# FFN down products on one core: W2's two parts as one 256-column operand, and two sums per row tile on VectorE

## What is computed

```python
logits = xt @ Wr + br
top_p, top_idx = jax.lax.top_k(jax.nn.softmax(logits, axis=-1), 2)
weights = top_p / top_p.sum(axis=-1, keepdims=True)
xn = (xt - mu) * jax.lax.rsqrt(var + LN_EPS)
xe = xn[None, :, :] * ln_g[:, None, :] + ln_b[:, None, :]
h = jax.nn.gelu(jnp.einsum('end,edh->enh', xe, W1) + b1[:, None, :], approximate=False)
y = jnp.einsum('enh,ehd->end', h, W2) + b2[:, None, :]
out = (weights[:, :, None] * sel).sum(axis=1)      # sel: y of the two chosen experts
```

## Time and profile before

| | us |
|---|---|
| median of 3 runs | 1040.82 (1039.2 to 1045.29) |
| the profiled execution | 1043.44 |
| its span | 1041.4 |
| TensorE busy (matmul) | 791.3 |
| VectorE busy | 631.6 |
| ScalarE busy | 583.3 |
| GpSimd busy | 560.8 |

### The profile page before, as it was taken

How to read it: one execution, slowest core, us unless ns; L and a number is a source line. 1 busy time by engine, 2 the same in 40 slices (tenths; PEclk the granted TensorE clock), 3 DMA queues, 4 the chain that set the end, 5 groups by cost and what they waited for, 6 DMA issues and landing times. The chain is left out here.

```text
span 1041.4 us, 25571 instructions
## 1 busy us (share of the span) xinstructions
PE 791.3 (76%) x7318; PEld 665.7 (64%) x7319; DVE 631.6 (61%) x2144; ACT 583.3 (56%) x1167; POOL 560.8 (54%) x581
## 2 busy tenths in 40 slices
PE   0667798687778377629278999999968899899995
PEld 0455688466668266512067877888757788787874
DVE  3555511877450588863257777878745666666663
ACT  1467752788332355231056766777646667676763
POOL 0756600443127788677725555656554555555554
PEclk9999999566579567555579999999998999999998
DMA  9497511566102244715123333333323333434441
GB/s 238 104 271 243 162 53 44 185 179 199 41 14 78 95 126 135 233 46 193 51 79 117 120 103 121 115 116 112 109 66 108 109 112 111 113 109 116 115 116 35
DMA packets 123849, 124.78 MB, mean 120 GB/s; under 512 B 22233, under 2 KB 91120, under 8 KB 123796
## 3 DMA queue, kind: packets, MB, share of 16 engines
q1 hardware_dynamic: 89476, 80.65, 27.3%
q0 software_dynamic: 15296, 34.64, 9.5%
q10 hardware_dynamic: 19024, 8.86, 3.0%
HBM read 77.40 MB, written 49.09 MB: 121 GB/s over the span
## 5 line engine op out<-in xcount | busy, mean ns | idle before, releaser
L1026 DVE TENSOR_TENSOR AB<-AB 128x512 f16<-128x512 f32 x280 | 192.1, 686 | 73.0 <-ACT AB L694 68.7
L528 POOL DMA_INDIRECT row_dram<-B x140 | 143.7, 1027 | 112.6 <-DVE B L1032 77.0
L528 POOL DMA_INDIRECT out<-B x140 | 139.6, 997 | 117.5 <-DVE B L1032 92.1
L691 ACT ACTIVATE AB<-ps 128x512 f16<-128x512 f32 x280 | 168.2, 601 | 41.2 <-PE ps L1208 40.6
L1225 PE MATMUL ps<-PPb,AB 128*128 x1120 | 185.3, 219 | 0.0
L1226 PE MATMUL ps<-PPb,AB 128*128 x1120 | 185.1, 219 | 0.0
L694 ACT ACTIVATE AB<-ps 128x512 f32<-128x512 f32 x280 | 169.2, 604 | 0.0
L1206 PE MATMUL ps<-B,PPb 128*128 128x256 f16 x560 | 154.5, 276 | 0.5 <-issue 0.5
L1207 PE MATMUL ps<-B,PPb 128*128 128x256 f16 x560 | 154.0, 275 | 0.0
L1208 PE MATMUL ps<-B,PPb 128*128 128x256 f16 x560 | 154.0, 275 | 0.0
L1228 PE MATMUL ps<-PPb,AB 128*128 x1120 | 153.9, 219 | 0.0
(11 more groups left out here) (218 smaller groups left out, 1620.9 us busy)
## 6 DMA issues: line engine op xcount, KB each, us to landing
B<-row_dram SPq DMA_DIRECT2D x70, 264.0 KB
B<-row_dram SPq DMA_DIRECT2D x70, 136.0 KB
rows<-in_x SPq DMA_DIRECT2D x32, 256.0 KB, 5.3
rows<-in_L_conv_protein_pair SPq DMA_DIRECT2D x16, 512.0 KB, 4.9
g_dram<-work ACTq DMA_DIRECT2D x32, 256.0 KB, 3.3
work<-g_dram SPq DMA_DIRECT2D x32, 256.0 KB, 2.8
ABT<-in_x SPq DMA_DIRECT2D x32, 256.0 KB, 3.0
ABT<-in_L_conv_protein_pair SPq DMA_DIRECT2D x16, 512.0 KB, 4.8
```

Source lines behind the costliest of these rows:

```text
L528: pool.indirect_dma_start(out_rows if second else row2_dram, bass.IndirectOffsetOnAxis(ap=Rw[:, u, b, at:at + 1].bitcast(u32), axis=0), Rw ...
L691: act.activation(Hp[:, hs, 0, :], ps[HB[hs]][:, :], ACT.Gelu, scale=1.0 / SCALE)
L1026: dve.tensor_tensor(Hp[:, hs, 1, :], Hf[:, q, :], Hp[:, hs, 0, :], ALU.subtract).then_inc(h_parts[q], 1)
```

## The change

The two parts of W2 are laid side by side for every piece k, so that one slice of 256 columns holds high and low. In the down block, for each k and half, the high part of the hidden layer is loaded once and streams all 256 columns into the whole width of 256 of bank 4 + b: the first 128 columns collect high x high, the second 128 high x low. The low part of the hidden layer streams the first 128 columns as before. That is 16 products in place of 24; the b2 products stay, now behind the first product of their bank. The bank then holds two sums. VectorE adds the first to the row in mix, as before, and the second in a new mix_low; y_high orders the two, and y_done is now released by mix_low. The order of VectorE's stages changes: both mix ahead of the second h_low, both mix_low behind it.

```diff
-        W2h = flat[:, 4096:8192].bitcast(f16).rearrange("p (e r k d) -> p e r k d", e=NE, r=2, k=HC)
+        W2h = flat[:, 4096:8192].bitcast(f16).rearrange("p (e k r d) -> p e k r d", e=NE, r=2, k=HC)
...
-        y_psum, y_done = ([sem(f"{name}{b}") for b in range(HALVES)] for name in ("y_psum", "y_done"))
+        y_psum, y_high, y_done = ([sem(f"{name}{b}") for b in range(HALVES)] for name in ("y_psum", "y_high", "y_done"))
...
-                        a = act.activation(W2h[:, e, 0, :, :], W2s[:, e, :, :], ACT.Copy, scale=SCALE)
+                        a = act.activation(W2h[:, e, :, 0, :], W2s[:, e, :, :], ACT.Copy, scale=SCALE)
...
-                i = dve.scalar_tensor_tensor(W2h[:, e, 1, :, :], W2s[:, e, :, :], SCALE, W2h[:, e, 0, :, :], ALU.mult, ALU.subtract)
+                i = dve.scalar_tensor_tensor(W2h[:, e, :, 1, :], W2s[:, e, :, :], SCALE, W2h[:, e, :, 0, :], ALU.mult, ALU.subtract)
...
                 dve.scalar_tensor_tensor(Rw[:, u, b, 0:D], ps[4 + b][:, 0:D], Rw[:, u, b, w:w + 1], Rw[:, u, b, 0:D],
+                                         ALU.mult, ALU.add).then_inc(y_high[b], 1)
+
+            def mix_low(n, u, second, b):
+
+                dve.wait_ge(y_high[b], n + 1)
+                w = WHI if second else WLO
+                dve.scalar_tensor_tensor(Rw[:, u, b, 0:D], ps[4 + b][:, D:2 * D], Rw[:, u, b, w:w + 1], Rw[:, u, b, 0:D],
                                          ALU.mult, ALU.add).then_inc(y_done[b], 1)
...
-                            (2, lambda n, u, second: h_low(n, u, 1)), (3, lambda n, u, second: mix(n, u, second, 1))], 2)
+                            (3, lambda n, u, second: mix(n, u, second, 1)), (2, lambda n, u, second: h_low(n, u, 1)),
+                            (3, lambda n, u, second: mix_low(n, u, second, 0)), (3, lambda n, u, second: mix_low(n, u, second, 1))], 2)
...
                 for b in range(HALVES):
                     if not isinstance(n, int) or n >= 1:
                         pe.wait_ge(y_done[b], n)
-                    pe.matmul(ps[4 + b][:, 0:D], allone[:, :], b23[:, bass.ds(x_ * D, D)], start=True, stop=False)
...
-                    w = lambda r: W2h[:, bass.ds(x_, 1), r, k, :].rearrange("p a d -> p (a d)")
+                    w = lambda parts: W2h[:, bass.ds(x_, 1), k, 0:parts, :].rearrange("p a r d -> p (a r d)")
...
                     for b in range(HALVES):
-                        pe.matmul(ps[4 + b][:, 0:D], hk(0, b), w(0), start=False, stop=False)
-                        pe.matmul(ps[4 + b][:, 0:D], hk(1, b), w(0), start=False, stop=False)
-                    for b in range(HALVES):
-                        i = pe.matmul(ps[4 + b][:, 0:D], hk(0, b), w(1), start=False, stop=(k == HC - 1))
+                        pe.matmul(ps[4 + b][:, 0:2 * D], hk(0, b), w(2), start=(k == 0), stop=False)
+                        if k == 0:
+                            pe.matmul(ps[4 + b][:, 0:D], allone[:, :], b23[:, bass.ds(x_ * D, D)], start=False, stop=False)
+                        i = pe.matmul(ps[4 + b][:, 0:D], hk(1, b), w(1), start=False, stop=(k == HC - 1))
```

## The result

The changed kernel takes **1070.21 us** (median of 4 runs, 1068.15 to 1074.86), beside 1042.63 us of the kernel before on the same chip. The ratio is 1.0273, with a 95% interval of 1.0239 to 1.0306: slower by 28 us. The profiled execution took 1074.86 us with a span of 1072.8, which is 31.4 more than the span of before (1041.4).

The account below looks back on a forecast made before the run. First list: two paths of nearly one length, TensorE's and the six-slot row-tile ring; 19 + 1 + 1 = 21 us on the profiled 1043.44 gave 1064.4, 2.6 above the median, so 1062 us; range 1045 to 1080.

Parts of the forecast that it names:

- Sums: 1.13 us later: VectorE's sums per tile: y_done of half 0 released 1.13 us later, that of half 1 0.53 later.
- First list's ring: Six row-tile slots, first list: store, load and norm move 1.13 us per turn; +0.30 per step, 19 us in all.
- Products: 0: TensorE's down block: merged products stream the same 3072 columns, 1.32 us per tile before and after; gain 0.
- Faster: Rival: down block's queued work covers more issue gap ahead of the transposes, step 3.35 us, 1021 us; chance 0.05.
- Weight loads count: Rival: saved weight loads in the down block gain 0.34 us per tile, second list 24 us, 1038 us; chance 0.03.
- TensorE's wait, "hidden by a hair": Second list's down block: weight load due 1.85 us after the sum, y_done at 1.74, load 0.04 later; 0.07 left.
- both lists: Rival: sum chain 0.1 us longer, the 0.07 us cover goes, second list pays 14 us too: 1076 us; chance 0.12.
- Second list's ring: +1: Second list's row-tile slots: one in three transposes waits 0.1 to 0.3 us for its load; +1 us, 3.5 at most.
- Ends: +1: Last tile of each list: four sums in a row make stores 0.52 us later, twice; +1 us.
- VectorE's load: First list: two more sums add 0.52 us per tile, about 3.3 of the 3.48 us step, so it fits.

Follow-up runs that it names:

- Eight slots: The changed kernel with eight slots for row tiles in place of six: 1044.11 us, ratio 1.0011 to the kernel before.
- the sums alone: The kernel before, its 24 products kept, with two added sums per tile (bank times 0) that release y_done, in the change's order: 1064.59 us.
- the products alone: The changed kernel with VectorE's order and two sums per tile as before, high x low sum left out of the row: 1023.22 us.
- the products alone with eight slots: Merged products without the second sums, with eight row-tile slots in place of six: 990.56 us, ratio 0.9491 to the kernel before.
- all sums first and eight slots: The changed kernel with all four sums ahead of the second h_low and eight row-tile slots in place of six: 993.38 us, ratio 0.9515.
- eight slots alone: The kernel before with eight slots for row tiles in place of six: 1036.94 us, ratio 0.9932.
- sums first without them: The changed kernel with all four sums ahead of the second h_low, still six row-tile slots: 1036.85 us, ratio 0.9949.

## Why the prediction was right, and where not

The forecast was 1062 us in a range of 1045 to 1080, slower with a chance of 0.80. Measured were 1070.21 us, on that side and in that range, but 0.2 us above the forecast's own range (1054 to 1070): 28 us more than before, where the sum had 21. The first list's loss came by the mechanism forecast. The second list came out as forecast by luck, since a loss and a gain that the prediction had not counted cancelled there; and the ends were mis-sized. Step by step:

- *Sums: 1.13 us later.* Right to the hundredth: 643.25 to 644.38. The first store came 2.29 us after the sum, in the forecast's 1.9 to 2.3.
- *First list's ring.* Right in mechanism, a little short: forecast +0.30 per step and 19 us (ends 17 and 24), measured 3.49 to 3.81 and 22.0 us. The turn shown above is 11.12 us, near the 11.25 worked out; why the mean step is 3.81 and not its 3.71 was not taken apart. The load came 2.61 us after the store, as forecast, and the norm 2.50 after that, where the prediction called 2.6 the bound; the sum of the two is 0.12 us shorter, and it would have had to fall by 1.1 for the turn to take up the delay. Eight slots take the loss away, and the sums alone reproduce it.
- *Products: 0.* Right for the block and wrong for the step. In the changed kernel's down block the pitches are 0.055 and 0.11 us, as forecast:

```profile
642.39 0.27 PE L1232 MATMUL ps<-PPb,AB 128*128 x1
642.50 0.22 PE L1235 MATMUL ps<-PPb,AB 128*128 x1
642.56 0.27 PE L1232 MATMUL ps<-PPb,AB 128*128 x1
```

  But of the 0.4 us of idle time behind the block 0.18 or nothing was left, and the runs with the products alone price that at 20 us with six slots and 46 with eight. The prediction had this as a rival ("Faster") and put it aside because of the ring; that reason held for the sign and not for the second list, where the gain was real and was eaten. The rival "Weight loads count" has no support as it was put, inside the block: the pitches did not change. The products alone gave the second list 0.29 us per tile, near that rival's 0.34, but behind the block; whether fewer loads, fewer products or longer ones shorten the idle time there was not separated. The Trainium skill's figure for that rival ("TensorE: Matmul & The Clock Gate", Back-to-back issue gap) is some 81 ns per 128-column product in a stream in which each product has a load of its own. The rows still show 0.055 us, and the trace differs from it.

- *TensorE's wait, "hidden by a hair".* This step failed. The weight load was to follow y_done by 0.04 us. In the turn above, the two low sums end at 644.98, and the block's first weight load, kernel after, starts 0.21 later, as it does (0.20 to 0.22) in 27 of 28 such waits between 600 and 700 us:

```profile
645.19 0.10 PEld L1232 LDWEIGHTS ps<-PPb,AB 128*128 128x128 f16 x1 [0.56 <-issue]
```

  In the kernel before the 0.04 is there at one of the two waits. At the end of its first list the two sums of one tile, and the two weight loads of the next block that wait for them, are these:

```profile
770.49 0.35 DVE L1032 SCALAR_TENSOR_TENSOR B<-ps,B 128x128 f32<-128x128 f32 x1 [0.34 <-issue]
...
771.36 0.35 DVE L1032 SCALAR_TENSOR_TENSOR B<-ps,B 128x128 f32<-128x128 f32 x1
```

```profile
770.99 0.10 PEld L1217 LDWEIGHTS ps<-AB,allone 128*128 128x128 bf16 x1 [0.66 <-issue]
771.75 0.10 PEld L1217 LDWEIGHTS ps<-AB,allone 128*128 128x128 bf16 x1 [0.67 <-DVE B L1032]
```

  Half 1's load starts 0.04 us behind its sum (771.71), and its wait stands at the product itself; half 0's starts 0.15 behind its sum (770.84; the row names issue), and its wait stands at the row ahead of it that prepares an address. The change moved both waits, and that for the first hidden group, to such a row ahead of the block, which the prediction did not count. That this is the whole of the 0.21 was not tested by itself.

  The chain sum to sum is 3.45 us (643.25 to 646.70), where the rival "Faster" had worked out 3.35. Since TensorE's own work needs only some 3.06 (the products alone with eight slots), the block waits in nearly every tile of the first list (by the list of waits above 22.9 us of idle matmul in 52 tiles, 0.44 us each, where 0.3 was forecast) and in more than half of those of the second (next row, 850 to 1020 us, 49 tiles):

```profile
PEld ps L1232 <- issue: 13.2, 29, 0.6
```

  The rival "both lists" named this loss, and the shorter idle time behind the block paid it back: the net is +1.0 us over 54 tiles.

- *Second list's ring: +1.* The number is right by luck, as the net of things that the step did not hold: the merged products' gain, the chain, and loads that come late.
- *Ends: +1.* Mis-sized: the change of lists with the 11 tiles behind it, and the last tiles with the end, cost 1.8 + 2.2 + 2.2 + 1.3 = 7.5 us. Of the 31.4 us between the two spans 22 are the first list, and this is most of the rest. The prediction priced only the last tile's four sums in a row, 0.52 us. At the end of the first list there are no transposes for three steps, and TensorE has less work of its own, but the chain is no shorter. VectorE's sums there, kernel after:

```profile
787.22 0.60 DVE L1032 SCALAR_TENSOR_TENSOR B<-ps,B 128x128 f32<-128x128 f32 x2
...
790.66 0.61 DVE L1032 SCALAR_TENSOR_TENSOR B<-ps,B 128x128 f32<-128x128 f32 x2 [0.73 <-PE ps L1235]
...
794.11 0.61 DVE L1032 SCALAR_TENSOR_TENSOR B<-ps,B 128x128 f32<-128x128 f32 x2 [0.82 <-PE ps L1235]
...
797.56 0.61 DVE L1032 SCALAR_TENSOR_TENSOR B<-ps,B 128x128 f32<-128x128 f32 x2 [1.72 <-PE ps L1235]
```

  They are 3.45 apart throughout, the bare chain. In the kernel before, the sums of half 0 of the same tiles are 3.17, 3.25 and 2.87 apart (764.07, 767.24, 770.49, 773.36). That is 1.05 us, and with the 0.52 of the four sums in a row it makes 1.6 of the 1.8. The last 2.2 are two loads that came late; in the kernel before, no transposes of the last three tiles waited for one:

```profile
1047.56 0.20 PEld L1191 LDWEIGHTS ps<-ident,B 128*128 128x128 f32 x2 [1.39 <-DMA B<-row_dram]
1051.22 0.20 PEld L1191 LDWEIGHTS ps<-ident,B 128*128 128x128 f32 x2 [0.71 <-DMA B<-row_dram]
```

  Why just these came late is open, and so is what makes up the 2.2 us of the 11 tiles at the begin of the second list.

- *VectorE's load.* About 3.3 us per step was too high; in the kernel with all sums first and eight slots 3.07 us hold all of it. It was not the bound of the changed kernel, whose first list has VectorE busy for 34.07 of 40 us.

## What to carry to other kernels

When one result is made by two instructions, the order in which the last of them stands decides, since everything behind the result waits for that one: with another instruction in the middle of its four sums the changed kernel is 28 us slower than the kernel before, without it 6 faster. An engine that is 93% busy may owe the rest to one short gap per step, and what removes that gap may be worth nothing, or less than its size, until the next limits (here a ring of six slots and the release of the banks) are met in the same change: the three edits together give 50 us, while eight slots alone give 6 and sums first without them 6. Where two limits are nearly equal, removing one shows no gain, and that is no proof that it does not bind.

## What the runs showed of the hardware

The idle time behind a register load on TensorE was not expected to behave as it did: it keeps its length wherever the load stands (0.23 to 0.25 us of idle matmul ahead of the transposes, 0.25 behind them), two transposes ahead of it hide none of it, and a down block of 16 products (half of them 0.11 us long) in place of 24 hides half (0.18 of 0.42 left in the weight loads' rows) to all of it: with six of the long products at its end, undisturbed rows show none. That TensorE's instruction stream gets ahead of the array while the long products run would fit, since eight products that are each 0.055 us longer give it 0.44 us; this was not measured by itself, and it is an explanation, not a finding. Nor had I expected that a weight load follows the sum it waits for by 0.04 us in one place and by 0.15 to 0.21 in another, or that TensorE and VectorE can both be busy for 99% of a stretch (39.55 and 39.94 of 40 us) although each needs the other's results in every step.
